# Sixteen-head attention: the scores of unit k are issued at the top of its step on TensorE

## The reference

```
x = x + L0_xattn(layernorm(x), ctx)      # single-head cross attention
x = x + L0_attn(layernorm(x))            # causal attention
x = x + L0_ffn(layernorm(x))             # quantised feed-forward
x = x + L1_xattn(layernorm(x), ctx)      # 16-head cross attention, heads of width 16
x = x + L1_attn(layernorm(x))            # local attention, window 2
x = x + L1_ffn(layernorm(x))             # 8 experts, top 2
```

```
qh = einsum(q, wq) + bq;  kh = einsum(kv, wk) + bk;  vh = einsum(kv, wv) + bv   # per head
attn = softmax(qh @ kh.T / sqrt(16));  ctx = attn @ vh
out = ctx.reshape(b, sq, 256) @ wo.T + bo
```

## Time and profile before

| | |
|---|---|
| median of 3 runs | 1964.88 us (1962.65 to 1965.19) |
| the profiled execution: its own time | 1961.54 us |
| the profiled execution: span from first to last instruction | 1959.7 us |
| PE busy | 90% of the span |
| DVE, ACT, POOL busy | 55%, 44%, 33% |
| mean granted TensorE clock | 0.955 of 2.4 GHz |

### The profile page before, as it was taken

How to read it: one execution, slowest core, us unless ns; L and a number is a source line. 1 busy time by engine, 2 the same in 40 slices (tenths; PEclk the granted TensorE clock), 3 DMA queues, 4 the chain that set the end, 5 groups by cost and what they waited for, 6 DMA issues and landing times. The chain is left out here.

```text
span 1959.7 us, 43596 instructions
## 1 busy us (share of the span) xinstructions
PE 1763.4 (90%) x12680; PEld 1443.3 (74%) x12713; DVE 1072.6 (55%) x3790; ACT 855.4 (44%) x2361; POOL 642.7 (33%) x1186
## 2 busy tenths in 40 slices
PE   3799999999999999999999999883599999999990
PEld 2477777767776776777777777762599999999990
DVE  4567766767676776776777777766311111111115
ACT  0466655656565665665665666641111111111110
POOL 0234333433343333433343334330133333333320
PEclk7899999999999999999999999995699999999996
DMA  9522322222222222222222221005544555455547
GB/s 326 209 74 86 97 66 80 86 79 85 78 87 78 89 75 83 83 87 76 82 82 85 80 82 37 6 12 204 186 173 178 187 185 175 177 185 184 179 146 263
DMA packets 124402, 235.82 MB, mean 120 GB/s; under 512 B 14448, under 2 KB 76400, under 8 KB 114096
## 3 DMA queue, kind: packets, MB, share of 16 engines
q1 hardware_dynamic: 117392, 214.87, 32.9%
q0 software_dynamic: 6816, 18.62, 2.5%
HBM read 203.16 MB, written 30.28 MB: 119 GB/s over the span
## 5 line engine op out<-in xcount | busy, mean ns | idle before, releaser
L725 ACT ACTIVATE x_prob<-ps,x_nmax 128x257 f32<-128x257 f32 x512 | 238.6, 472 | 237.5 <-DVE x_nmax L1026 237.1
L1413 ACT ACTIVATE heT<-ps 128x512 f32<-128x512 f32 x142 | 84.8, 597 | 441.3 <-PE ps L1379 441.3
L447 PE MATMUL ps<-context,x_probT 128*128 128x128 f32 x2048 | 275.4, 278 | 0.9 <-ACT x_probT L719 0.8
L1379 PEld LDWEIGHTS ps<-xeT,w_block 128*128 128x128 f32 x2272 | 266.2, 193 | 12.8 <-issue 8.5
L1379 PE MATMUL ps<-xeT,w_block 128*128 128x128 f32 x2272 | 266.9, 276 | 8.6 <-DMA w_block<-in_m_w 8.1
L447 PEld LDWEIGHTS ps<-context,x_probT 128*128 128x128 f32 x2048 | 259.6, 194 | 10.7 <-issue 2.5
L1365 PE MATMUL ps<-w,heT 128*128 x1136 | 256.8, 379 | 0.0
L1365 PEld LDWEIGHTS ps<-w,heT 128*128 128x128 f32 x1136 | 210.4, 190 | 25.7
L1026 DVE TENSOR_REDUCE x_nmax<-ps 128x1 f32<-128x257 f32 x512 | 192.1, 415 | 40.2 <-PE ps L612 40.2
L719 ACT ACTIVATE x_probT<-ps 128x512 f32<-128x512 f32 x224 | 133.7, 597 | 146.0 <-PE ps L606 142.9
L790 POOL TENSOR_TENSOR x_lastv<-context,x_prob 128x128 f32<-128x128 f32 x256 | 120.4, 470 | 227.3 <-ACT x_prob L725 227.3
(11 more groups left out here) (269 smaller groups left out, 3131.1 us busy)
## 6 DMA issues: line engine op xcount, KB each, us to landing
w_block<-in_m_w SPq DMA_DIRECT2D x71, 1024.0 KB, 4.8
context<-in_cT SPq DMA_DIRECT2D x128, 257.0 KB, 2.9
context<-in_cn SPq DMA_DIRECT2D x128, 256.0 KB, 3.0
context<-in_lastk SPq DMA_DIRECT2D x128, 128.0 KB, 3.6
yrows<-zero SPq DMA_DIRECT2D x1, 8192.0 KB, 30.3
w<-in_m_w SPq DMA_DIRECT2D x8, 1024.0 KB, 12.5
w<-yrows SPq DMA_DIRECT2D x16, 512.0 KB, 6.0
xin<-in_x SPq DMA_DIRECT2D x32, 128.0 KB, 3.1
```

The source lines that it names most:

```text
L447: t = mm(out, a, b, start=n == 0, stop=n == len(pairs) - 1)
L725: A(p1[kk % 2][:, g, :], ps[:, g, 0:KEYS], ACT.Exp, bias=nmax1[kk % 2][:, g:g + 1], accum_out=rsum1[kk % 2][:, g:g + 1]).then_inc(e1_ok.ha ...
L1379: t = mm(ps[:, 2 * b + n, f * P:(f + 1) * P], w1[b][:, k, lo:lo + P], xeT[b][:, k, :], start=k == 0, stop=k == H - 1)
L1413: A(heT[b][:, n * FK // 2:(n + 1) * FK // 2, :].rearrange("p k t -> p (k t)"), ps[:, 2 * b + n, :], ACT.Gelu).then_inc(heT_ok.handle, 1)
```

## The change

On PE, `unit_scores` of unit k is issued as the first thing of step k, ahead of `unit_probs_T` of unit k - 1 and of the even position; before, it came behind both. So that banks 0 and 1 are not overwritten while ACT still reads them, each of the two products now waits on `e1_ok` of unit k - 1; before, the wait of `unit_probs_T` ahead of it covered that. Nothing else is changed on any engine.

```diff
@@ unit_scores
                 if k == 0 and g == 0:
                     W(pe, pool_s["query1"], t, "blocks")
+                if not (isinstance(K, int) and K == 0):
+                    W(pe, e1_ok, K - 1, g + 1)
                 mm(ps[:, g, 0:KEYS], qblk[m % 2][...], cT[m][...], start=True, stop=True).then_inc(s1_ps.handle, 1)
@@ slot
                     last, older, oldest = sl.half(k - 1), sl.half(k - 2), sl.half(k - 3)
+                    if sl.half(k):
+                        for g in (0, 1):
+                            unit_scores(*sl.half(k), g)
                     if last:
                         unit_probs_T(*last, oldest if oldest and oldest[2] % 2 == 1 else None)
                     sl.steps(table, 2 * k)
-                    if sl.half(k):
-                        for g in (0, 1):
-                            unit_scores(*sl.half(k), g)
                     if older and older[2] % 2 == 1:
                         unit_fold(*older, last or older)
                     sl.steps(table, 2 * k + 1)
```

## The result

The changed kernel takes 2040.59 us at the median (2039.66 to 2044.65), the kernel before 1964.74 in the same runs: 1.0392 times as long, interval 1.0374 to 1.041. That is +76 us; the forecast was +56, in a range of +32 to +79.

What follows compares the result with a forecast made beforehand. PE's closed row of instructions, busy 90% of the span, bounds the kernel; lost cover of 1.87 us a slot costs 54 us in 29 slots plus 3 in the last three, +57, giving 2021 us (range 1997 to 2044).

Steps and rivals of the forecast that it cites:

- The shift of 0.72 us: Top of each step on PE: transposes and even position come 0.72 us later, as weight loads are not pulled ahead.
- The new waits at the top cost nothing: Added `e1_ok` waits on the scores cost nothing, since the transposes waited for the same signal at the same place.
- step 5: Only `s0_out` covers the copy; late `x_prob` now met in the scores; chain through cross0's softmax to `query_norm`: loss 0.56 us.
- step 4: `c0_scores(1)` with `ff_down` in the even position cover the copy: loss 0.
- Step 2: ACT's copies of self0's q, k, v end later, so `s0_scores` starts at 801.14, not 801.00: loss 0.14 us.
- Step 6: Copy covered by `c0_values(0)` and `q1_q`, but one change of shape more: loss 0.09 us.
- Step 7: `c0_attT` and `ro_logits` last 0.65 us; the fold comes at 825.65, not 825.27: loss 0.38 us.
- Step 1: Scores were the only cover of DVE's copy; the fold and DVE's row behind it come later: loss 0.63 us.
- Rival 1 (faster): The scores' head start reaches the exponentials and removes PE's stalls: 1960 us, or 1936 with the gaps; chance 0.06.
- 2 (no change): Hidden slack behind each stall makes up lost cover, or waits were equal before: 1965 us; chance 0.04.
- 3 (a smaller loss): Weight loads are pulled past the scores, or only one step hurts: 0.6 us a slot, 1984 us; chance 0.07.
- Rival 4, the clock: Longer gaps in step 1 take PE's clock down in each slot, another 54 us: 2075 us; chance 0.03.

Runs made afterwards that it cites:

- experiment 1: Changed kernel with the scores of step 1 alone put back behind the even position: 2015.07 us, 1.025 times before.
- experiment 2: Kernel before, with the scores ahead of the transposes in step 1 alone, new waits in every step: 1991.18 us, 1.0129 times.
- experiment 7: Kernel before, with the scores moved behind the transposes but ahead of the even position, no waits added: 1970.41 us, 1.0026 times.
- experiment 5: Changed kernel with a single unread product of 512 columns in the wait of step 1: 2028.82 us.
- experiment 3: Changed kernel with eight unread transposes of the identity between the transposes and the fold of step 1: 2039.96 us.

## Why the prediction was right, and where not

Step by step, as it put them:

- **What bounds: PE's closed row.** Held; the busy time of PE grew through overlap and the clock, the number of instructions is the same.
- **The shift of 0.72 us.** It measured 0.64 (749.65 to 750.29) and about 0.1 ahead of it. The rows had been read rightly: the weight load of the transposes is not pulled past the scores of 64 rows. PEld stands idle for "issue" ahead of L606, 26.3 us in 76 times between 600 and 1000 us. Before, that row had only two restarts (6.8 us in 2), and the idle time stood ahead of what followed the scores then (L447 and L620, 26.4 us in 87). The prediction had set this against the Trainium skill, TensorE: Matmul & The Clock Gate, "Part 3: Packing small matmuls", which says that a weight load overlaps matmuls in flight only when its row group differs. That opposition was too sharp: the same section speaks of row groups that don't conflict, and a load for all 128 rows takes in the 64 of the scores. Where the trace does differ from that sentence is between products of one shape: at 817.34 us the load of the values starts together with a product of the same 128 rows and 0.11 us ahead of its own.

The waits of PEld, changed kernel, 600 to 1000 us:

```profile
PEld ps L606 <- issue: 26.3, 76, 0.7
```

- **The new waits at the top cost nothing.** Wrong in step 5. Top of step 5 in the changed kernel:

```profile
818.44 1.02 PE L614 MATMUL ps<-context,query_blocks 64*128 64x257 f32 x4
...
818.51 0.20 ACT L727 ACTIVATION_READ_ACCUMULATOR x_prob<-ps,x_nmax 128x1 f32 x1
...
819.39 0.66 PE L606 MATMUL ps<-constants,x_prob 128*128 128x128 f32 x4
```

From the scores to the transposes it is 0.95 us, elsewhere 0.64. The late signal (818.71) was there before and cost the transposes about 0.15; in front of the second product of the scores it costs 0.31. The single records show why. The two products of a unit lie in different halves of the 128 rows, and elsewhere they run side by side: at 749.65 us their first records start 0.007 us apart. So the second product meets the wait at once: in step 5 the first starts at 818.44 and the second at 818.76, just behind the signal. The second pair of transposes would have started only 0.22 us behind the first, and so met the same lateness when most of it was over. That is the 0.28 by which step 4 in the table is longer, a step that I put at 0.
- **Step 0:** 0.14, not 0.07. **Step 2:** 0.21, not 0.14. **Step 3:** 0.05 shorter, said no change. **Step 6:** 0.15, not 0.09. **Step 7:** 0.41, not 0.38.
- **Step 1:** 0.49 by the table, 0.60 from top to fold, said 0.63. Experiments 1 and 2 bear the mechanism out.
- **Step 5:** 0.51, said 0.56, and by the chain that was named:

```profile
820.09 0.60 ACT L721 ACTIVATE x_probT<-ps 128x512 f32<-128x512 f32 x1 [0.95 <-PE ps L606]
...
821.17 0.16 DVE L878 RECIPROCAL cross_rinv<-cross_rsum 128x1 f32<-128x1 f32 x1 [0.89 <-ACT cross_prob L668]
...
821.83 0.44 PE L455 MATMUL ps<-constants,query_norm 128*128 128x128 f32 x2 [0.20 <-DVE query_norm L858]
```

The copy holds up the softmax of cross0 on ACT, that one DVE's inverse and `query_norm`, and PE waits for `query_norm`; in the earlier trace rows nothing waited there. The chain even gave some back: `query_norm` takes 0.50 us here, 0.62 in the earlier trace rows, and so in every full slot.
- **Sum:** said 1.87 a slot, measured about 2.15. Over 32 slots that is 9 of the 20 us that were missing. Nearly all of it is the 0.28 at the top of step 5. By its own sign ("in size if steps 3, 4 or 6 lengthen") the prediction was off in size: step 4 lengthened by this, step 6 by 0.15.
- **Rival 1 (faster), 2 (no change) and 3 (a smaller loss):** out. The head start does not reach the next wait of PE (experiment 7).
- **Rival 4, the clock:** the step that failed. I gave it 0.03 and put "gaps of 0.3 to 0.5 leave the clock at 0.99" against it, but the gap of step 1 was going to be 0.9, with 0.45 behind it, and no row of before had such a pair. It came in every fourth slot, not in each, and cost 12 us, not 54. Experiment 5 shows that PE's standing still in step 1 is needed for these falls: with the first gap filled they are gone, and the 12 us with them. It isn't enough, as the other seven slots with the same gaps and experiment 1 show. What decides between slots is open; so is the part of the second gap, which no experiment took away alone in the changed kernel. The Trainium skill, TensorE: Matmul & The Clock Gate, "HAM oscillation", has idle gaps in a loop take the clock down each time round, there with waits for transfers that are longer than these. This trace agrees in so far as each of the loop's seven rounds of four slots has one fall, always at the same place, with gaps of only 0.88 and 0.45 us; experiment 2 has its falls at changing places.

Together the 9 and the 12 us are the 20 that were missing, as nearly as the restarts allow. That the time still lies in the range is in part luck: the upper end, 2044, was put for steps that might lose more, not for the clock, which was a rival with a time of its own, 2075. What the steps alone would have come to is near 2029, the time of experiment 5.

## What to carry to other kernels

Moving independent work ahead of a producer on the bounding engine takes it away from between that producer and its users: count for each user what is left between, for this is where such work was doing its good. A head start for an operation is worth something only if the next engine takes it up earlier, and with fixed orders on each engine that is read from what stands ahead of it there. A wait moved to another instruction is the same wait, but it can be met earlier: count from where its instruction could start. And when new idle time appears on TensorE, the forecast needs a term for the clock.

## What was unexpected of the hardware

- A wait of 0.88 us with 0.45 us more behind it in one step was followed by a fall of TensorE's clock in every fourth slot (0.66 granted over 5 us, 1.66 us lost each time); one unread product in the first gap kept it at 1.00 and was worth 12 us of 2041. The same pair left the clock alone in seven other slots of the same kernel, and 0.98 with 0.36 us did so in all seven slots of experiment 1 that have it.
- The gap at a restart of the loop was 2.2 to 3.5 us in most kernels and 4.0 to 4.7 at ten restarts in two of them, each time with a second 16 KB instruction fetch at its start. With 64 transposes put ahead of the loop, and the loop unchanged, it went from 23.3 to 16.1 us over six restarts. So such a gap can mask a change of a few instructions; experiment 3 by its total alone would have refuted the account of the clock.
- Two products of 64 rows in different halves of the array's rows started 0.007 us apart; in step 5, where the second had to wait for a signal 0.27 us late, they started 0.32 us apart.
